# Folded Fourier transforms, and a third of a short convolution moved to the matmul engine, in a hybrid block's long convolution

## The reference, cut to what matters

```python
x = x + attn_a(layernorm(x), ...)
# attn_a: b, l, d = 16, 256, 128
up = (u @ w_in + b_in).transpose(0, 2, 1)            # 128 -> 3 x 128 channels
uc = conv(up, sf_w, kernel 3, padding 2, per channel)[..., :l] + sf_b
x0, x1, v = split(uc, 3, axis=1)                     # x0: the gate
k = implicit_filter(...).T                           # a sine network, 512 positions
v = v * x1
y = irfft(rfft(v, n=2*l) * rfft(k, n=2*l), n=2*l)[..., :l]
v = y + v * filt_bias
out = (v * x0).transpose(0, 2, 1) @ w_out + b_out
```

## Time and profile before

| what | value |
|---|---|
| runs | 514.41, 515.03, 516.46 us |
| the profiled execution's own time | 516.48 us |
| its span in the profile | 514.6 us |
| mean granted TensorE clock | 0.981 of full speed |
| busy share of the span: PE / DVE / ACT / POOL | 92% / 71% / 53% / 64% |

### The profile page before, as it was taken

One profiled execution on the slowest core, in us unless ns is written; L12 is line 12 of the kernel. 1 busy time (PEld: TensorE's weight loads), 2 busy tenths in 40 slices (PEclk: granted clock), 3 DMA queues, 4 the chain that ended last, 5 costly groups with the idle time before them and its releaser, 6 DMA issues.

```text
span 514.6 us, 13024 instructions
## 1 busy us (share of the span) xinstructions
PE 471.2 (92%) x3852; PEld 367.3 (71%) x3852; DVE 364.7 (71%) x1136; ACT 270.8 (53%) x716; POOL 327.0 (64%) x446
## 2 busy tenths in 40 slices
PE   3989999999899999996899999999889999999994
PEld 1658878787665999974576676666677656999962
DVE  6688999967766656544877787878877766566635
ACT  3464444653561555544667676676765542555530
POOL 4455766648772466651798899999746771566640
PEclk9999999998999999999999999999979999999997
DMA  8999950001111233316000000000001111333229
GB/s 280 325 383 406 403 225 1 0 2 41 48 54 47 73 85 95 84 52 165 0 3 3 2 3 2 4 1 3 2 14 36 53 53 47 84 83 95 78 73 291
DMA packets 36993, 47.56 MB, mean 92 GB/s; under 512 B 4186, under 2 KB 28123, under 8 KB 36798
## 3 DMA queue, kind: packets, MB, share of 16 engines
q1 hardware_dynamic: 31648, 35.90, 21.4%
q0 software_dynamic: 4544, 9.35, 5.3%
q10 hardware_dynamic: 734, 1.50, 1.0%
HBM read 17.86 MB, written 28.87 MB: 91 GB/s over the span
## 4 chain that ended last, share of the span: by engine, by line
PE 74%; DVE 10%; ACT 8%; issue 5%; POOL 1%; DMA 0%; ACTq 0%; DVEq 0%; POOLq 0%
PE bank L783 69%; ACT silu_sh L1249 2%; PE bank L305 2%; PE bank L893 2%; DVE prod L1614 2%; ACT rows L1242 1%; ACT scores_odd L1224 1%; ACT wide L1224 1%; DVE conv_xv L1521 1%; ACT k_tok L1224 1%; PE bank L1179 1%; PE bank L795 1%; DVE residual L1620 1%; DVE prod L1791 1%; PE bank L992 1%
## 5 line engine op out<-in xcount | busy, mean ns | idle before, releaser
L660 POOL DMA_INDIRECT routed<-row_out,row_token x78 | 74.9, 960 | 66.4 <-DVE row_token L1682 49.9
L783 PE MATMUL bank<-row_in_t,row_weights 128*128 128x128 f32 x624 | 84.0, 278 | 1.9 <-issue 1.2
L783 PEld LDWEIGHTS bank<-row_in_t,row_weights 128*128 128x128 f32 x624 | 75.7, 192 | 4.2 <-issue 2.8
L651 POOL DMA_INDIRECT sorted_rows<-rows,place x64 | 62.3, 973 | 23.0 <-issue 14.3
L1290 ACT ACTIVATE row_silu<-bank 128x256 f32<-128x256 f32 x78 | 29.9, 383 | 48.2 <-PE bank L783 48.2
L1674 DVE TENSOR_SCALAR row_weights<-experts 128x512 f32 x78 | 33.9, 435 | 26.9 <-issue 23.2
L783 PE MATMUL bank<-wide,weights_sb 128*128 128x512 f32 x112 | 51.5, 597 | 0.0
L783 PE MATMUL bank<-experts,row_act 128*128 x312 | 50.1, 283 | 1.3 <-ACT row_out L1224 1.1
L1249 ACT ACTIVATE silu_sh<-bank 128x512 f32<-128x512 f32 x32 | 19.0, 594 | 60.0 <-PE bank L783 59.8
L1666 DVE TENSOR_TENSOR row_act<-row_silu,bank 128x256 f32<-128x256 f32 x78 | 32.8, 420 | 19.8 <-ACT row_silu L1290 10.9
L1224 ACT ACTIVATE wide<-bank 128x512 f32<-128x512 f32 x54 | 29.4, 592 | 30.8 <-PE bank L783 17.1
(11 more groups left out here) (194 smaller groups left out, 1092.2 us busy)
## 6 DMA issues: line engine op xcount, KB each, us to landing
sorted_rows<-zeros SPq DMA_DIRECT2D x1, 17028.0 KB, 50.6
row_in<-sorted_rows SPq DMA_DIRECT2D x78, 64.5 KB
rows<-routed SPq DMA_DIRECT2D x8, 256.0 KB, 4.9
scores_odd<-routed SPq DMA_DIRECT2D x8, 256.0 KB, 5.3
out<-residual SPq DMA_DIRECT2D x8, 256.0 KB, 3.6
routed<-row_out,row_token POOLq DMA_INDIRECT x78, 2.3
tables_sb<-tables SPq DMA_DIRECT2D x1, 1024.0 KB, 8.8
experts<-rt_gate SPq DMA_DIRECT2D x1, 1024.0 KB, 18.4
```

The lines of the kernel that those rows point to most:

```text
L651: pool.indirect_dma_start(sorted_rows, bass.IndirectOffsetOnAxis(ap=place[:, t:t + 1].bitcast(U32), axis=0), rows[:, t, :], None).then_inc ...
L660: pool.indirect_dma_start(routed, bass.IndirectOffsetOnAxis(ap=row_token[:, r:r + 1].bitcast(U32), axis=0), row_out[:, r, :], None).then_i ...
L783: return pe.matmul(out_, lhsT, rhs, start=start, stop=stop, **kw)
```

## The change

**Folded transforms.** For each sequence of 256 steps the value is folded about its middle, 127.5: v[t] + v[255-t] and v[t] - v[255-t] for t < 128. The cosine part of the transform (with its phase taken from the middle) needs the sum alone, the sine part the difference alone. The forward transform becomes 4 matmuls of 256 columns with new tables; the inverse gives an even and an odd half of 128 steps, each from 2 matmuls of 128 columns for each sequence (8 in all), and the output is even + odd and, backwards, even - odd. The filter's own spectrum is made as before.

**The gate third.** From pair 2 on (BY_MATMUL = 2) the three taps of third 0 are three matmuls that accumulate in bank 1, with weights w_in times the tap, over the tokens shifted by 0, 1 and 2 steps. ScalarE copies the bank with a bias; for steps 0 and 1 of each sequence it uses biases of their own, in copies of 2 x 1 elements. VectorE leaves third 0 out. The weights are made once, by VectorE after short_conv(0), from a row of taps that a new DMA on ScalarE's queue spreads over all partitions (128 x 1536 bytes); a small step is added to the bias table.

**The order.** GpSimd's value waits for its own product and does the two folds, with one operand read backwards. ScalarE gets `copy_odd`, the odd half from bank 6 to SBUF, behind tap2 and ahead of conv_apply; VectorE's gate waits for that copy, does sum and difference to out_c in SBUF, waits for them, and multiplies out_c by the gate: both inputs of L1799's successor are now in SBUF. keep(2) and scale_rows(1) move from first_silu to a part of their own ahead of copy_odd. forward(0) waits for the table load that inverse(0) waited for; the load has the size it had. scores_odd, a tile of the attention, holds the new temporaries.

```diff
             def value(k):
-                pool.wait_ge(c_conv, 3 * k + 2)
+                pool.wait_ge(c_conv, convolved(k, 1))
+                pool.tensor_tensor(value_c[:], conv_xv[:, 0, :], conv_xv[:, 1, :], ALU.mult).then_inc(c_value, 1)
+                pool.wait_ge(c_value, k + 1)
                 wait(pool, c_value_turned, k)
-                pool.tensor_tensor(value_c[:], conv_xv[:, 0, :], conv_xv[:, 1, :], ALU.mult).then_inc(c_value, 1)
+                v = value_c[:].rearrange("p (b t) -> p b t", b=2)
+                folded = value_fold.rearrange("p (b h t) -> p b h t", b=2, h=2)
+                for h, op in enumerate((ALU.add, ALU.subtract)):
+                    pool.tensor_tensor(folded[:, :, h, :], v[:, :, 0:P], v[:, :, L - 1:P - 1:-1], op).then_inc(c_folded, 1)
...
                 for n, g in enumerate(THIRDS):
-                    wait(pe, c_conv, 3 * (k - 1) + n + 1)
-                    mm(pe, bank[1 + g][:], w_in_sb[:, g * D:(g + 1) * D], normed_t[:]).then_inc(c_proj, 1)
+                    if g or k <= BY_MATMUL:
+                        wait(pe, c_conv, convolved(k - 1, n))
+                    else:
+                        pe.wait_ge(c_tap2, tapped(k))
+                    if g or k < BY_MATMUL:
+                        mm(pe, bank[1 + g][:], w_in_sb[:, g * D:(g + 1) * D], normed_t[:]).then_inc(c_proj, 1)
+                        continue
+                    if k == BY_MATMUL:
+                        pe.wait_ge(gate_weights_made, 1)
+                    o, n_t = (a[:].rearrange("p (b t) -> p b t", b=2) for a in (bank[1], normed_t))
+                    for late in range(3):
+                        last = mm(pe, o[:, :, late:L], gate_weights[:, 2 - late, :], n_t[:, :, 0:L - late],
+                                  start=(late == 0), stop=(late == 2), skip_group_check=True)
+                    last.then_inc(c_proj, 1)
...
-                        for s in range(SB):
-                            last = mm(pe, o, dft[:, s, c, f * P:(f + 1) * P], v[:, s, :, :],
-                                      start=(s == 0), stop=(s == SB - 1))
+                        last = mm(pe, o, fold_dft[:, c, f * P:(f + 1) * P], v[:, c, :, :])
...
-                            last = mm(pe, bank[6][:, b * L:(b + 1) * L], y[:, c, f, b, :], inverse_dft[:, c, f, :],
-                                      start=(c == 0 and f == 0), stop=(c == 1 and f == FB - 1))
+                            last = mm(pe, bank[6][:, b * L + c * P:b * L + (c + 1) * P], y[:, c, f, b, :],
+                                      inverse_dft[:, c, f, :], start=(f == 0), stop=(f == FB - 1))
...
+            def copy_odd(k):
+                act.wait_ge(c_inverse, k + 1)
+                copy(act, out_odd, bank[6][:].rearrange("p (b h t) -> p b h t", b=2, h=2)[:, :, 1, :]).then_inc(c_odd_copied, 1)
...
+                    if g == 0 and k >= BY_MATMUL:
+                        dst, src = (a.rearrange("p (b t) -> p b t", b=2)
+                                    for a in (gates[:, bass.ds(k * PT, PT)], bank[1][:]))
+                        for of, bias in ((slice(2, L), conv_bias[:, 0:1]), (slice(0, 1), gate_edge[:, 0:1]),
+                                         (slice(1, 2), gate_edge[:, 1:2])):
+                            act.activation(dst[:, :, of], src[:, :, of], ACT.Identity, bias=bias).then_inc(c_tap2, 1)
+                        continue
...
-                       (2, each(tap2)), (3, each(conv_apply)), (3, each(copy_normed)),
+                       (2, each(tap2)), (0, beside({7: third_keep})), (0, each(copy_odd)), (3, each(conv_apply)),
+                       (3, each(copy_normed)),
...
+            def scale_gate_weights():
+                dve.wait_ge(gate_taps_loaded, 16)
+                dve.tensor_tensor(gate_weights, w_in_sb[:, 0:D].unsqueeze(1).to_broadcast([P, 3, D]),
+                                  gate_tap_rows.rearrange("p (k d) -> p k d", k=3), ALU.mult).then_inc(gate_weights_made, 1)
...
             def gate(k):
-                dve.wait_ge(c_inverse, k + 1)
+                dve.wait_ge(c_odd_copied, k + 1)
+                even = bank[6][:].rearrange("p (b h t) -> p b h t", b=2, h=2)[:, :, 0, :]
+                y = out_c.rearrange("p (b t) -> p b t", b=2)
+                dve.tensor_tensor(y[:, :, 0:P], even, out_odd, ALU.add).then_inc(c_unfolded, 1)
+                dve.tensor_tensor(y[:, :, L - 1:P - 1:-1], even, out_odd, ALU.subtract).then_inc(c_unfolded, 1)
+                dve.wait_ge(c_unfolded, 2 * (k + 1))
                 wait(dve, c_out, k)
-                dve.tensor_tensor(gated[:], bank[6][:], gates[:, bass.ds(k * PT, PT)], ALU.mult).then_inc(c_gated, 1)
+                dve.wait_ge(c_tap2, tapped(k + 1))
+                dve.tensor_tensor(gated[:], out_c, gates[:, bass.ds(k * PT, PT)], ALU.mult).then_inc(c_gated, 1)
```

More of the change, by code:

```diff
@@ L113, in shape_constants @@
     weight = np.where(np.arange(NF // 2) == 0, 1.0, 2.0) / NF
-    inv = (dft[:L] * weight).transpose(1, 2, 0)
-    c["inverse_dft"] = inv.reshape(2, FB, P, L).transpose(2, 0, 1, 3)
+    centred = np.arange(P)[:, None] - (L - 1) / 2
+    fold_cos, fold_sin = np.cos(2 * np.pi * centred * f / NF), -np.sin(2 * np.pi * centred * f / NF)
+    fold_sin[:, 0] = -np.sin(np.pi * centred[:, 0])
+    fold = np.stack([fold_cos, fold_sin], 1)
+    c["fold_dft"] = fold
+    inv = (fold * weight).transpose(1, 2, 0)
+    c["inverse_dft"] = inv.reshape(2, FB, P, P).transpose(2, 0, 1, 3)
     c["identity"] = np.eye(P)
@@ L140, in hybrid_block @@
 def hybrid_block(nc, x, weights, filter_weights, f_w1, filt_bias, b_out, rt_gate, rt_up, rt_down,
-                 tables, positions, out):
+                 tables, positions, gate_taps, out):
     with ExitStack() as ctx:
@@ L172, in hybrid_block @@
         dft = table("dft", "p (t c f) -> p t c f", t=TAU, c=2)
+        fold_dft = table("fold_dft", "p (c f) -> p c f", c=2)
         inverse_dft = table("inverse_dft", "p (c f t) -> p c f t", c=2, f=FB)
@@ L318, in hybrid_block @@
         edge_tmp = sb("edge_tmp", [P, 3, 2])
+        gate_edge = sb("gate_edge", [P, 2])
         conv_xv = sb("conv_xv", [P, 2, PT])
         value_c = sb("value_c", [P, PT])
+        scores_odd = sb("scores_odd", [P, 2 * HEADS * P])
+        value_fold = scores_odd[:, 0:PT]
+        out_odd = scores_odd[:, PT:PT + 2 * P].rearrange("p (b t) -> p b t", b=2)
+        out_c = scores_odd[:, 2 * PT:3 * PT]
+        gate_tap_rows = scores_odd[:, 3 * PT:3 * PT + 3 * D]
+        gate_weights = scores_odd[:, 4 * PT:4 * PT + 3 * D].rearrange("p (k d) -> p k d", k=3)
         value_t = sb("value_t", [P, PAIR, D])
@@ L336, in hybrid_block @@
         c_value = sem("c_value")
+        c_folded = sem("c_folded")
+        c_odd_copied = sem("c_odd_copied")
+        c_unfolded = sem("c_unfolded")
+        gate_taps_loaded = sem("gate_taps_loaded")
+        gate_weights_made = sem("gate_weights_made")
         c_value_turned = sem("c_value_turned")
@@ L997, in forward @@
                 wait(pe, c_prod, 4 * k)
-                v = value_t[:].rearrange("p (b s) d -> p s b d", s=SB)
+                if k == 0:
+                    pe.wait_ge(inverse_loaded, 16)
+                v = value_t[:].rearrange("p (b h) d -> p h b d", h=2)
                 for c in range(2):
@@ L1388, in third_apply, with third_keep, first_silu @@
                 early_apply(2)
-            def first_silu():
+            def third_keep():
                 keep(2)
                 scale_rows(1)
+            def first_silu():
                 silu_half(0, 0)
@@ L1772, in short_conv @@
                 for n, g in enumerate(THIRDS):
-                    dve.wait_ge(c_tap2, 3 * k + n + 1)
+                    if g == 0 and k >= BY_MATMUL:
+                        continue
+                    dve.wait_ge(c_tap2, tapped(k) + n + 1)
                     dst = seqs(conv_xv[:, g - 1, :] if g else gates[:, bass.ds(k * PT, PT)])
@@ L1988, with convolved, tapped @@
 THIRDS = (1, 2, 0)
-EDGE_STEPS = 7
+def convolved(k, n):
+    return 3 * min(k, BY_MATMUL) + 2 * max(k - BY_MATMUL, 0) + n + 1
+def tapped(k):
+    return 3 * min(k, BY_MATMUL) + 5 * max(k - BY_MATMUL, 0)
+BY_MATMUL = 2
+EDGE_STEPS = 8
 FLT_LAYER = 3
@@ L2023 @@
         "rt_gate": L0_ffn_rt_gate, "rt_up": L0_ffn_rt_up, "rt_down": L0_ffn_rt_down,
-        "tables": tables, "positions": positions}
+        "tables": tables, "positions": positions,
+        "gate_taps": np.asarray(L0_attn_a_sf_w)[0:D].reshape(D, -1).T.reshape(-1)}
     arrays = {name: np.ascontiguousarray(a) for name, a in arrays.items()}
```

19 lines of the change are left out of this document (11 added, 8 removed).

## The result

| | before | after |
|---|---|---|
| median of 20 runs each, us | 516.70 (514.41 to 517.98) | 512.49 (510.73 to 515.27) |
| profiled span, us | 514.6 | 510.9 |
| mean granted clock in it | 0.981 | 0.976 |

The ratio is 0.9929 [0.9917, 0.9941] (in brackets the 95% interval): faster by 4.2 us, under 1% but clear of the noise, where 7.1 were forecast. Of the 4.6 us between the forecast's 507.9 and the median, 1.7 are the before that it started from (three runs at 515.03; twenty at 516.70), 2.9 are the change.

A forecast was written before the change was run, and what follows sets the result against it. TensorE and VectorE were both taken as full. Iteration 0 -0.7, iterations 1 to 4 -1.6, iteration 5 -1.15, iterations 6 and 7 -3.65: in all -7.1 from 515.03, forecasting 507.9 us, range 503.5 to 512.5.

The forecast's parts named there:

- the start of iteration 0: Folds delay turn_value(1) and project(2) takes 1.7 longer, yet add_conv(0) comes at 44.4 for 45.08: -0.7 us.
- the weights' multiplication: VectorE's one multiplication making the gate weights after short_conv(0), 0.42 to 0.69 us, falls in a wait and costs nothing.
- Rival D: TensorE's granted clock falls to 0.50 in each iteration; decides from period 12.9, two falls; 519.5 us; chance 0.08.
- Block of the multiplication: VectorE's multiplication, both inputs in SBUF, waits for GpSimd's value: a 0.64 us stall each iteration, about 1.3 long.
- rival A: The multiplication is not held by GpSimd; period 10.3, or 10.5 by the ring of waits; 504.9 us; chance 0.18.
- Period: Loop iteration on VectorE: 10.3 of its own work plus 0.64 stall, 10.94 us for 11.33; iterations 1 to 4 save 1.6.
- Rival B: Backward accesses are dear: folds of 1.27, differences of 0.69; the loop saves nothing; 510.8 us; chance 0.18.
- Ring and GpSimd: Chain of waits across engines over two iterations, 21.6 us, 10.8 each; two GpSimd folds of 0.77, queue behind hardly moves.
- Iteration 5: No conv_stats_in (1.22 less), but the small step L1776 may be held 0.45: 10.17 us for 11.33, -1.15.
- Iterations 6 and 7: Shorter transforms, table load behind copy_odd: add_conv(6) 10.7 after add_conv(5), project_out(7) at 17.4 for 21.07, -3.65 us.
- Carried whole: Stages after the pipeline start earlier by about the same, so the whole 7.1 us gain reaches the end.
- rival C: The pipeline ends earlier but GpSimd's sends or the row tiles' start lose it; under 2.6 us arrive; 513.8; chance 0.09.

The follow-up runs named there:

- e3: Changed kernel with 12 matmuls of no use behind conv_turn(2), in TensorE's pause for the folds of pair 1: 509.73 us, ratio to before 0.9856.
- e1: Changed kernel with sum and difference written back to PSUM bank 6, so the multiplication has one SBUF input: 512.03 us, ratio to before 0.9894.
- e4: Changed kernel with GpSimd's out_bias cut from 128 x 512 to 128 x 4 elements: 512.34 us, ratio to before 0.9908, period still 10.67.
- e5: Changed kernel with ScalarE's table load and scale_rows(0) of iteration 6 put ahead of copy_odd(6): 513.25 us, ratio to before 0.9938.
- e12: The changed kernel once more, unaltered: 513.01 us, ratio to before 0.9927.
- e2: Changed kernel with project(2) ahead of turn_value(1) on TensorE and tap2(2) ahead of copy_value(1) on ScalarE: 510.44 us, ratio to before 0.9859.
- e10: Changed kernel with the edits of e1 and e2 together, no useless work: 508.96 us, ratio to before 0.9858.
- e11: Changed kernel with e1's edit, e3's 12 useless matmuls and 9 more in TensorE's pause of iteration 6: 508.08 us, ratio to before 0.9837.

## Why the prediction was right or wrong

- **What failed: the start of iteration 0.** The prediction had the folds delay turn_value(1) and project(2), and priced project(2) at 2.4 GHz: "-0.7". Measured +2.2. The pause of 2.99 us that the delay makes on TensorE was never written down, so its price, a granted clock of 0.50 over project(2), was left out. e3 keeps the delay and takes away the pause: add_conv(0) is 2.3 earlier, which is most of the 2.9 that the start missed by. The other 0.6, as far as the traces can say, is a term put at nothing: the weights' multiplication "falls ahead of a wait of VectorE for project(1): nothing". It took 1.02, not 0.42 to 0.69, and by way of GpSimd's queue it made the value of pair 1 0.76 late. Rival D named the clock, but looked for falls inside the loop (period 12.9), where in the profile of after there was none.
- **Block of the multiplication: right.** 1.16 to 1.20 long, ending 0.55 behind value, for 1.3 and 0.6. e1 removes it and gets 10.31, the 10.3 of rival A.
- **Period: right in mechanism, 10.67 for 10.94.** Four products and the way to add_conv take 2.39 (55.54 to 57.93) for the 2.57 of the earlier trace rows, and the multiplication 1.09 to its successor (54.45 to 55.54) for 1.24. That gave 1.0 more over four iterations. Rival B is refuted: folds 0.71 each, differences 0.41.
- **Ring and GpSimd.** That its queue "hardly moves" was too light: it is full in after. It costs nothing yet (e4).
- **Iteration 5: the number is right (9.98 for 10.17), one of its waits by luck.** The small step was held as forecast (0.59 at 93.50). The multiplication, forecast as held, was not (0.69); VectorE waited 0.51 for copy_odd instead.
- **Iterations 6 and 7: 18.14 for 17.4.** The table load stands where it was put and the chain is the forecast's, each step a little later: the router's matmuls end at 9.28 for 8.9, and add_conv(6) is at 11.26 for 10.7. But no single step can be said to hold it: e5 moved the load and shifted the wait to VectorE's order.
- **Carried whole: not quite.** project_out(7) is 4.7 earlier, the first transposition of the row tiles 4.45 (162.34 for 166.79), the end 3.7. In between the clock falls at other places than before (360 to 375: 0.89 for 1.00). e12, the same kernel, has 0.77 there, and falls at 124 to 132 as well. It is the loss of rival C in kind, at 1.0 us; how much of it is the clock stays open.

Most of the runs' spread goes with the clock. The 20 runs of after, ordered by time, with each one's mean granted clock (the fastest five and the slowest five):

```
510.73 0.978  510.86 0.978  510.92 0.978  511.11 0.978  511.12 0.980
513.93 0.967  514.82 0.968  514.90 0.968  514.99 0.968  515.27 0.968
```

The means of the two rows are 510.9 and 514.8 us; in e1's and e3's four runs each the order by clock is the order by time. The kernel before stays at 0.980 to 0.987 in 26 runs beside the experiments. A likely reading, not tested for the later stages, is that the change leaves TensorE pauses behind which the clock falls in some runs and not in others.

## What to carry to other kernels

When a change frees the engine that was full, write down every pause it gets and how long it is, first at the pipeline's start, where no other work stands beside it: the wait may cost nothing and the half clock behind it 2 us. Move work ahead into the pause (e2, e10). Two edits that each relieve one engine and load another can be slower alone (1.011 and 1.017) and faster together (0.993), so price them as one sum. And a tile that lies in PSUM already is the better second operand beside a busy GpSimd: in e1's profile it saved 0.36 us an iteration, for a changed address and one wait.

## What the runs showed of the hardware

- An operand read backwards on GpSimd, or a result written backwards by VectorE, cost nothing that the traces show: two folds of 128 x 256 back to back took 1.42, 0.71 each, beside 0.77 for a plain product; 0.41 for the backward difference beside 0.42 for the sum.
- The block between VectorE and GpSimd goes both ways, and a small step pays it too: one of 32 elements a partition took 1.14 in e5, and two folds took 1.75 for 1.42.
- Pauses of 2.99 and 3.13 us on TensorE were followed by a granted clock of 0.50 in both profiles of this kernel, and pauses of 2.70 to 3.17 at the same place in e1, e4 and e5; a pause of 2.20 was followed by it in four profiles and not in four others. With matmuls whose result nobody reads (2.84 us of them in e3, 2.17 in e11) in the pause it was 1.00. In e11 no stretch of 4 us was below 1.00 before 232, but neither was one in e10, which leaves the second pause unfilled.
